# Local attention in another order: the work of each engine in a tile moved, half of the weighing one step later, and a subtraction made by scalar_tensor_tensor

## The reference, cut to what matters

```python
h = shift_token(x)                 # second half of the values from the token before
q, k, v = jnp.split(h @ wqkv, 3, axis=-1)
q = l2norm(q) * qs
k = l2norm(k) * ksc
q, k = rotary_xpos(q, k)           # q * cos * scale + rotate_half(q) * sin * scale, k with 1 / scale
# local_attention: each window of 128 queries sees its own keys and those of the window before
sim = jnp.einsum('bhwid,bhwjd->bhwij', bq, bk)
mask = (i < j) | (i > j + WINDOW) | (j == -1)
sim = jnp.where(mask, -jnp.finfo(sim.dtype).max, sim)
attn = jax.nn.softmax(sim, axis=-1)
out = jnp.einsum('bhwij,bhwjd->bhwid', attn, bv)
x = x + o @ wo
```

## Time and profile before

| | |
|---|---|
| time, median of 3 runs | 4296.58 us (4293.78 to 4302.39) |
| the profiled execution | 4296.06 us, its span 4294.4 us |
| mean granted clock of TensorE | 0.951 of full |
| PE busy | 3835.2 us, 89% |
| DVE busy | 3330.0 us, 78% |
| ACT busy | 2558.9 us, 60% |
| POOL busy | 1191.1 us, 28% |

### The profile page before, as it was taken

One profiled execution on the slowest core, in us unless ns is written; L12 is line 12 of the kernel. 1 busy time (PEld: TensorE's weight loads), 2 busy tenths in 40 slices (PEclk: granted clock), 3 DMA queues, 4 the chain that ended last, 5 costly groups with the idle time before them and its releaser, 6 DMA issues. The chain is left out here.

```text
span 4294.4 us, 94790 instructions
## 1 busy us (share of the span) xinstructions
PE 3835.2 (89%) x38292; PEld 2167.2 (50%) x38292; DVE 3330.0 (78%) x5467; ACT 2558.9 (60%) x3449; POOL 1191.1 (28%) x966
## 2 busy tenths in 40 slices
PE   7999999769998969998986999999999999866996
PEld 4788888535655535555553332332333333334664
DVE  5688988779985569985687889999998978584444
ACT  3566666646553435653443777787888887744553
POOL 1022321267761067771141000000000000033552
PEclk9999999889999989999997999999999999977998
DMA  1010100133330033430072000000000000034664
GB/s 63 5 40 28 43 25 25 41 70 64 63 51 28 0 63 66 65 55 9 0 160 47 9 9 2 9 2 2 9 2 2 9 2 9 4 100 93 117 134 111
DMA packets 325878, 175.39 MB, mean 41 GB/s; under 512 B 239508, under 2 KB 316520, under 8 KB 324968
## 3 DMA queue, kind: packets, MB, share of 16 engines
q1 hardware_dynamic: 302856, 133.88, 14.8%
q0 software_dynamic: 13440, 21.24, 2.9%
q10 hardware_dynamic: 9184, 14.68, 1.4%
HBM read 77.81 MB, written 38.58 MB: 27 GB/s over the span
## 5 line engine op out<-in xcount | busy, mean ns | idle before, releaser
L2257 DVE TENSOR_REDUCE s_tops<-ps 128x2 f32<-128x1024 f32 (+3 forms) x1152 | 1252.2, 1132 | 143.2 <-PE ps L2143 103.6
L2226 ACT ACTIVATE s_weights<-ps 128x1024 f32<-128x1024 f32 (+3 forms) x1152 | 1092.5, 952 | 344.3 <-PE ps L2156 193.8
L2178 PE MATMUL ps<-s_weights,v_flat 128*32 128x256 f32 (+1 forms) x8704 | 692.1, 390 | 7.4 <-ACT s_o_t L2232 6.1
L2137 PE MATMUL ps<-keys,s_q 48*128 48x512 f16 (+3 forms) x2304 | 435.0, 375 | 46.0 <-DVE s_tops L2257 26.0
L2156 PE MATMUL ps<-s_q,keys 50*128 50x512 f16 (+3 forms) x2304 | 434.0, 374 | 46.9 <-DVE s_tops L2257 33.3
L2293 POOL CAST s_shift<-s_minus_top 128x16 f16<-128x16 f32 x32 | 6.3, 196 | 1429.9 <-DVE s_minus_top L2264 1429.9
L583 PE MATMUL ps<-a_qt,a_kt 128*128 128x256 f16 x3072 | 375.3, 273 | 3.8 <-POOL s_ones L538 3.8
L2156 PEld LDWEIGHTS ps<-s_q,keys 50*128 50x128 f16 x2304 | 112.2, 93 | 512.3 <-issue 246.7
L1174 PE MATMUL ps<-attention_w,la_yt 128*128 128x512 f16 x1152 | 289.3, 399 | 37.8 <-DMA la_yt<-la_y_parts 30.3
L583 PEld LDWEIGHTS ps<-a_qt,a_kt 128*128 128x128 f16 x3072 | 300.9, 98 | 40.3 <-POOL s_ones L538 4.2
L1249 ACT ACTIVATE la_weights<-ps 128x1024 f32<-128x1024 f32 x124 | 126.8, 1023 | 291.5 <-PE ps L1164 291.5
(11 more groups left out here) (372 smaller groups left out, 7158.0 us busy)
## 6 DMA issues: line engine op xcount, KB each, us to landing
ex_whole<-in_L_ffn_w_dram ACTq DMA_DIRECT2D x14, 1024.0 KB, 10.2
qk_parts<-a_parts SPq DMA_DIRECT2D x64, 128.0 KB, 4.3
keys<-qk_parts SPq DMA_DIRECT2D x48, 128.0 KB, 5.7
s_q<-qk_parts SPq DMA_DIRECT2D x48, 128.0 KB, 5.0
x<-in_x_dram SPq DMA_DIRECT2D x8, 512.0 KB, 9.3
attention_w<-attention_split SPq DMA_DIRECT2D x2, 2048.0 KB, 9.1
la_table<-in_rotary_dram SPq DMA_DIRECT2D x64, 64.0 KB, 2.1
a_table<-in_rope_dram POOLq DMA_DIRECT2D x8, 512.0 KB, 6.1
```

Source lines behind the costliest of these rows:

```text
L2137: mm = pe.matmul(m.ps[:, bank, 0:width], b.q[rows(half, KEY_PARTS * L1_DH), place % 2, pair, t * P:(t + 1) * P], m.keys[rows(half, KEY_PAR ...
L2178: mm = pe.matmul(m.ps[h * QUAD:(h + 1) * QUAD, OUT, begin:end], m.v_flat[:, first:first + QUAD], weights[:, a % 2, h, begin:end], start=(k ...
L2226: act.activation(weights[:, a % 2, 2 * pair:2 * pair + 2, skip:CHUNK], m.ps[:, bank:end + 1, skip:CHUNK], ACT.Exp).then_inc(s["exp"], 1)
L2257: dve.tensor_reduce(tops[:, u % 2, :, i % 2, t, c], m.ps[:, bank:end + 1, 0:width], AX.X, ALU.max).then_inc(s["max"], 1)
```

## The change

Only the `step` functions of `local_attention` and two operations change:

- PE: `project_q`, `project_k` of a tile come a step earlier and stand last in the step; `weigh(w, 1)` comes a step later, as the second thing of step w + 1, and `project_o` a step later, as the first. `find(i + 2, 1)` moves behind `score(i, 1)`. Between `score(i, 0)` and `score(i, 1)` now stands only `project_v(i + 1)`.
- DVE: `low` and `sums` of a tile come a step later, `divide(w, 0)` too; `rotate` now stands between the two `find`s, and `low` is the first call of a step, behind `find(i + 2, 1)` of the step before.
- `take_shift` goes from DVE to ACT.
- POOL: `add` and `norms` of a tile a step later, right ahead of `normalise`.
- SP: `turn_shift`, `turn_k`, `turn_q` and `place_shift` each work on one tile less ahead. The order in SP's step stays.
- `low` is a scalar_tensor_tensor (times 1.0, minus the high half) instead of a tensor_tensor.
- There is one more step at the end, and the row statistics that hang on a number of finished tiles come a step later.

The diff:

```diff
@@ -931,7 +931,7 @@
     near = m.mask[:, :, :].rearrange("p b k -> p (b k)")
     wqkv = m.attention_w[:, :, 0:KD * 3 * INNER].rearrange("p s (k e) -> p s k e", k=KD)
     wo = m.attention_w[:, :, KD * 3 * INNER:].rearrange("p s (k e) -> p s k e", k=INNER // P)
-    LOAD, HALF_ROWS, DOWN, ROWS, POWER, UP = 2, EARLY_TILES + 1, EARLY_TILES + 2, EARLY_TILES + 4, EARLY_TILES + 5, EARLY_TILES + 6
+    LOAD, HALF_ROWS, DOWN, ROWS, POWER, UP = 2, EARLY_TILES + 2, EARLY_TILES + 3, EARLY_TILES + 5, EARLY_TILES + 6, EARLY_TILES + 7
     early = slice(0, EARLY_TILES)
     with ExitStack() as ctx:
         def sb(name, shape, dt=F32):
@@ -966,7 +966,7 @@
 
         def run(step):
 
-            for i in range(-7, TILES + 2):
+            for i in range(-7, TILES + 3):
                 step(i)
 
         def after(eng, sem, n):
@@ -1036,13 +1036,13 @@
                 def step(i):
                     if exists(i + 5):
                         load_table(i + 5)
+                    if exists(i + 1):
+                        turn_shift(i + 1)
                     if exists(i + 2):
-                        turn_shift(i + 2)
-                    if exists(i + 3):
-                        turn_k(i + 3)
-                        turn_q(i + 3)
-                    if exists(i + 2):
-                        place_shift(i + 2)
+                        turn_k(i + 2)
+                        turn_q(i + 2)
+                    if exists(i + 1):
+                        place_shift(i + 1)
                     if exists(i + 6):
                         turn_y(i + 6)
                     if i == LOAD:
@@ -1108,19 +1108,18 @@
                     pool.tensor_tensor(rnorm[:, :], ss[:, :], m.minus_half[:, 0:2 * HEADS], ALU.pow).then_inc(s["rnorm"], 1)
 
                 def step(i):
-                    if exists(i + 3):
-                        normalise(i + 3)
                     if exists(i + 4):
                         tables(i + 4)
+                    if exists(i + 5) and i + 5 and (i + 5) % RING == 0:
+                        edge(i + 5)
+                    if exists(i + 3):
+                        add(i + 3)
+                        norms(i + 3)
+                        normalise(i + 3)
                     if exists(i - 1):
                         low_o(i - 1)
-                    if exists(i + 5) and i + 5 and (i + 5) % RING == 0:
-                        edge(i + 5)
                     if exists(i + 6):
                         low_y(i + 6)
-                    if exists(i + 4):
-                        add(i + 4)
-                        norms(i + 4)
                     if i == POWER:
                         rows_on_gpsimd(pool, m, s, 0)
 
@@ -1215,25 +1214,25 @@
                     mm.then_inc(s["proj"], 1)
 
                 def step(i):
+                    if exists(i - 2):
+                        project_o(i - 2)
+                    if exists(i - 1):
+                        weigh(i - 1, 1)
                     if exists(i + 2):
                         find(i + 2, 0)
-                    if exists(i + 4):
-                        project_q(i + 4)
                     if exists(i):
                         score(i, 0)
-                    if exists(i + 2):
-                        find(i + 2, 1)
-                    if exists(i + 4):
-                        project_k(i + 4)
                     if exists(i + 1):
                         project_v(i + 1)
                     if exists(i):
                         score(i, 1)
+                    if exists(i + 2):
+                        find(i + 2, 1)
+                    if exists(i):
                         weigh(i, 0)
-                    if exists(i - 1):
-                        project_o(i - 1)
-                    if exists(i):
-                        weigh(i, 1)
+                    if exists(i + 5):
+                        project_q(i + 5)
+                        project_k(i + 5)
 
                 run(step)
 
@@ -1283,29 +1282,36 @@
                     after(act, s["pv"], ROUNDS * (w - SLOTS + 2))
                     act.activation(v[:, w % SLOTS, :], m.ps[:, V_BANK, :], ACT.Copy, scale=1 / SCALE).then_inc(s["v"], 1)
 
+                def take_shift(w):
+                    act.wait_ge(s["top"], ROUNDS * (w + 1))
+                    after(act, s["shift_t"], 16 * (w - 1))
+                    act.activation(shift[:, w % 2, 0:HEADS], top[:, w % 2, :], ACT.Copy, scale=-1.0).then_inc(s["shift"], 1)
+
                 def high_y(w):
                     landed(act, y_in, w - 2)
                     act.copy(y_parts[:, w % 2, 0, :], m.y[:, w, :]).then_inc(s["y_high"], 1)
 
                 def step(i):
-                    if exists(i + 1) and i + 1:
-                        queries_for_before(i + 1)
+                    if exists(i - 1):
+                        soften(i - 1, 1)
+                    if exists(i + 4):
+                        square(i + 4)
+                    if exists(i + 7):
+                        high_y(i + 7)
+                    if exists(i + 3) and i + 3:
+                        keys_before(i + 3)
                     if exists(i):
                         soften(i, 0)
-                    if exists(i + 3):
-                        high(i + 3)
-                    if exists(i + 4):
-                        square(i + 4)
                     if exists(i - 1):
                         high_o(i - 1)
                     if exists(i + 1):
                         take_v(i + 1)
-                    if exists(i + 3) and i + 3:
-                        keys_before(i + 3)
-                    if exists(i):
-                        soften(i, 1)
-                    if exists(i + 7):
-                        high_y(i + 7)
+                    if exists(i + 3):
+                        high(i + 3)
+                    if exists(i + 2):
+                        take_shift(i + 2)
+                    if exists(i + 2) and i + 2:
+                        queries_for_before(i + 2)
 
                 run(step)
 
@@ -1316,6 +1322,7 @@
                 def find(w, r):
                     dve.wait_ge(s["found"], ROUNDS * w + r + 1)
                     after(dve, s["top"], ROUNDS * w + r)
+                    after(dve, s["shift"], w - 1)
                     first = 0 if w else P
                     for g in range(2):
                         for h in range(2):
@@ -1324,15 +1331,10 @@
                                                          1.0, -3e38, ALU.add, ALU.max, top[:, w % 2, n:n + 1])
                     t.then_inc(s["top"], 1)
 
-                def take_shift(w):
-                    dve.wait_ge(s["top"], ROUNDS * (w + 1))
-                    after(dve, s["shift_t"], 16 * (w - 1))
-                    dve.tensor_scalar(shift[:, w % 2, 0:HEADS], top[:, w % 2, :], -1.0, None, ALU.mult).then_inc(s["shift"], 1)
-
                 def low(w):
                     dve.wait_ge(s["high"], w + 1)
-                    dve.tensor_tensor(parts[:, w % 2, :, 1, :], straight[:, w % 2, :].rearrange("p (n e) -> p n e", n=2), parts[:, w % 2, :, 0, :],
-                                      ALU.subtract).then_inc(s["low"], 1)
+                    dve.scalar_tensor_tensor(parts[:, w % 2, :, 1, :], straight[:, w % 2, :].rearrange("p (n e) -> p n e", n=2), 1.0, parts[:, w % 2, :, 0, :],
+                                             ALU.mult, ALU.subtract).then_inc(s["low"], 1)
 
                 def rotate(w):
                     dve.wait_ge(s["squares"], w + 1)
@@ -1378,24 +1380,23 @@
 
                 def step(i):
                     if exists(i + 2):
-                        find(i + 2, 0)
+                        low(i + 2)
+                    if exists(i - 1):
+                        divide(i - 1, 0)
+                    if exists(i + 3):
+                        sums(i + 3)
+                    if exists(i - 3):
+                        halves(i - 3)
+                    if exists(i - 2):
+                        residual(i - 2)
                     if exists(i - 1):
                         divide(i - 1, 1)
                     if exists(i + 2):
-                        find(i + 2, 1)
-                        take_shift(i + 2)
-                    if exists(i + 3):
-                        low(i + 3)
+                        find(i + 2, 0)
                     if exists(i + 4):
                         rotate(i + 4)
-                    if exists(i):
-                        divide(i, 0)
-                    if exists(i + 4):
-                        sums(i + 4)
-                    if exists(i - 2):
-                        halves(i - 2)
-                    if exists(i - 1):
-                        residual(i - 1)
+                    if exists(i + 2):
+                        find(i + 2, 1)
                     if i == HALF_ROWS:
                         dve.wait_ge(s["six"], EARLY_TILES)
                         half_rows_on_vector(dve, m, s, 0)
```

## The result

The changed kernel takes 4450.9 us, the kernel before 4296.7 (medians of four runs each); the ratio over all these runs is 1.0363, 95% interval 1.0347 to 1.0380. It is 154 us slower, where 14 were forecast, and above the range. Nearly all of it is in local attention. From the first to the last score of a layer it takes 460.8 and 452.9 us, before 376.3 and 375.8: 161.6 of the 169.5 us by which the spans of the two profiled executions differ.

The account below looks back on a forecast made before the run. A closed loop over POOL's power, ACT's high and DVE was taken to set the 12.29 us tile. The new SP loop, 12.30 plus 0.4 for late DMAs, gives 12.7; with layer ends +6.8 per layer, +14 in all: 4310 us, range 4275 to 4400.

Parts of the forecast that it names:

- the new loop: Local attention, from score over second find, low, SP's turns and placing to next score: 12.30 us, 12.7 with late DMAs.
- PE's long wait: Sign at PE's score (L1159): waits for band about once a tile, by some tenths to over 1 us.
- Its wait for `la_o`: Sign on PE in the profile after: its wait for la_o is gone.
- race: DVE's low (wants to start at 5.50) against POOL's 2.37 us add (5.59); the sum has low win.
- the sum: Times added from the start of score(i, 0) to the next score, every DMA at its usual speed: 12.30 us.
- It is ahead by 0.09: On DVE and POOL, low at 5.50 us behind the score starts before the add at 5.59.
- Rival 1: Race lost: add first, k's turn on SP at 9.05 not 7.12, 1.93 a tile, 4422 (partly 4340 to 4420); chance 0.22.
- the sum had SP free at 5.89: On SP, the shift's turn starts 5.89 us behind the score, place_shift at 9.86.
- Late DMAs, 0.4 a tile: SP's queue in the loop: one k turn in three late by 0.87, plus late landings, together 0.4 us a tile.
- Ends: Ends of a local attention layer: first score 4.6 us earlier, the last step's low and turns cost about 1.
- scalar_tensor_tensor: no effect: DVE's low in the new form takes 1.23 us, not expected to differ, and is hidden either way.
- `take_shift` on ACT: The shift's write on ACT, without a row: taken as 0.19 us, bounded by 0 and 0.61.

Follow-up runs that it names:

- e5: The changed kernel with POOL's add waiting for low and POOL's low_y ahead of low_o: 4369.7 us, 1.0166 of the kernel before.
- e13: e1 with y's turn and the table's load behind the placing of band on SP, and ACT's high_y a tile earlier: 4357.4 us, 1.0144.
- e2: The changed kernel with eight more matmuls of 512 columns a tile ahead of PE's wait for the turned q: 4433.2 us, 1.0305.
- e1: The changed kernel with POOL's add of a tile waiting for low of the tile before: 4412.5 us, 1.0260 of the kernel before.
- e11: e5 with four more matmuls of 512 columns a tile ahead of PE's wait for the turned q: 4350.1 us, 1.0125.
- e4: The changed kernel with low as a tensor_tensor subtraction again: 4448.5 us, 1.0340 of the kernel before.
- e8: The kernel before with low by scalar_tensor_tensor alone: 4297.2 us, 1.0001 of the kernel before.
- e7: e5 with the second find ahead of the second score on PE, behind the projection of v: 4338.6 us, 1.0088.
- e14: e13 with the second find ahead of the second score and the MLP's loads two a step over four steps: 4327.9 us, 1.0083.
- e16: e14 with DVE's rotate ahead of divide(i - 1, 1) and the first find's maxima: 4311.2 us, 1.0023 of the kernel before.
- e6: The changed kernel with POOL's low_y ahead of low_o alone, the add not waiting for low: 4422.2 us, 1.0290.
- e9: e5 with the second find right behind the first score on PE, ahead of the projection of v: 4344.5 us, 1.0114.
- e10: e9 without POOL's wait for low ahead of the add: 4375.9 us, 1.0181 of the kernel before.

## Why the prediction was wrong, point by point

The direction and the new loop were right: POOL's power waits for DVE, and the loop runs from score over the second find, `low` and SP's queue to the next score. PE's long wait was expected at the score, for `band`; it stands just ahead, at the first find, for q's turn (25.4 us in 200, against 0.9 for `band`). Its wait for `la_o`, expected to go, fell only from 11.0 to 6.5. With race and y's turn out of the way (e5, e13) the loop takes 12.38 us against 12.30 in the sum.

- **The failed step is "It is ahead by 0.09".** The add starts where it was said, 5.59 behind the score. `low` starts at 5.60, not 5.50: from the first score to the next instruction it takes 1.29, where I took the 1.19 of the earlier trace rows. That row has a `find` behind the score; now a projection stands there. The kernel before shows the 1.29 too, where something else follows the score:

```profile
1016.95 0.60 PE L1160 MATMUL ps<-band,spread 128*128 128x256 bf16 x4
...
1018.24 1.08 PE L1205 MATMUL ps<-la_weights,la_v 128*32 128x128 f32 x32
```

It isn't PE's idle time ahead of the score: in e2 the extra matmuls leave none in half of the tiles, and it is 1.29 there as well. The race was lost by 0.00 to 0.02 in the quiet tiles, all but the two behind a copy for the ring's edge. Rival 1 was the case that happened, to the number in a quiet tile: k's turn was put at 9.05 and starts at 9.07. The total is another matter: rival 1 ended at 4422, and 29 more came from the terms below. The error was to give a difference of 0.09, under the spread of its own terms, a chance of only 0.22.
- **A second step failed with it: the sum had SP free at 5.89.** I counted y's turn and the table on SP, but not what releases them: `low_y`, now behind `low_o` on POOL and so behind exp. They move the shift's turn to 6.73, 0.84 a tile. Under the lost race it is hidden; e1 against e5 shows 43 us of it, and e13 against e1 55 by the other way. With the race won but this left as it was, e1 measures 4412.5, still over the range's 4400; e5, without both, has 4369.7 and lies in it. (The 0.03 by which the sum goes from 5.86 to 5.89 has no source either, and is of no weight.)
- **Late DMAs, 0.4 a tile**: in the 28 of the 46 tiles that run at the upper clock, the time from k's turn to the next score is 5.79 in the mean against 5.2 in quiet ones, so 0.59 a tile, where 0.4 was taken. It isn't at k's turn, which takes 1.24 to 1.26 throughout, but in landing: from the start of q's turn until PE has it, it takes 4.3 to 4.8 us in 12 of the 46 tiles and 3.2 to 3.9 in the others. Right in kind, a third too small, and at another DMA than the one that was read.
- **No term for the clock.** By the earlier trace rows it was 1.00 and I left it there, though the new loop makes PE wait before `find`. Taking it away brought 18 to 20 us, what the extra matmuls cost already taken off (e2, e11; e11 is the cleaner one, since it has no race).
- **Ends and the loads.** The first score comes at 911.76 against 911.84, not 4.6 earlier. The race eats that gain too: ahead of the first score `low` takes 3.14 at 890.90 and 2.23 at 904.32. In e1, where it takes 1.22 there, the first score comes at 907.54, 4.3 earlier than before. The first two intervals of a layer cost 11 us over both layers, the tiles with the loads another 11, both unforeseen.
- **scalar_tensor_tensor: no effect**, right (e4, e8). `take_shift` on ACT takes 0.21, where 0.19 was taken.

The account of the 154 as steps from kernel to kernel, each in the order in which it was taken: race 38 (e1), y's turn 43 (e5), second find 31 (e7), then 11 for SP's order and the split loads (e14), and 17 for e16, whose mechanism isn't shown. That is 140, from medians of different rounds (the kernel before has 4296.1 to 4299.7 in them). The rest of 14 (12 against the kernel before in e16's own runs, with a ratio of 1.0023) is open: e16 has a clock of 1.00 in the 200 us and still takes 12.6 a tile against 12.1 before. None of these steps can be read as its value in another order: race and y's turn hide each other (e1, e5, e6), and something on DVE hides the place of the second find (e7, e9); `rotate` stands there, but no run has it out of the way.

## What to carry to other kernels

When an edit breaks the loop that sets the time, list everything that the next instruction in line waits for, on every queue, and what releases each of those, since several may be late at the same place: here `low`, the add and the shift's turn behind y's turn all came due between 5 and 7 us behind the score (5.60, 5.59 and 6.73 in a quiet tile). Where two instructions that contend start within 0.1 us of each other by the sum, price both sides: here the coin fell the same way in 26 of the 28 tiles at the upper clock. Or order them by a wait, which here cost nothing: POOL's power waited 3.8 us for `la_ss` in the changed kernel, and in e1 it still waits 0.2 for it. Price a loop that has a DMA queue in it with its late landings: PE waited 25.4 us in 200 for q here, and 2.2 in the kernel before, whose turns ran a step further ahead. And read a row's distance to the next instruction only for the same next instruction: the 1.19 that was 1.29 lost the race.

## What the runs showed of the hardware that was not expected

- Which of `low` and the add pays changed over 0.10 us in e10: a `low` started 0.04 ahead of the add (1757.29 against 1757.33) takes 1.22 and the add 3.40, one started 0.06 behind it (1701.86 against 1701.80) takes 3.38 and the add 2.37. In the changed kernel a `low` started 0.01 behind the add (983.32 against 983.31) takes 3.44, and one started 0.11 ahead (1926.48 against 1926.59) takes 1.24 and the add 3.35.
- In the changed kernel PE fell to the lower level (a granted clock of 0.51 from 1072.20 to 1075.00) behind an idle stretch of 2.26 us, and the projection that followed took 2.74 for 1.47, while the mean clock of the 200 us still read 0.93. Four matmuls a tile whose results are thrown away gave more than they cost: e11, in which four take 1.04 us at 1036.00, measures 20 us less than e5.
- In the changed kernel the turn of q landed late in 12 of 46 tiles, 4.3 to 4.8 us behind its start instead of about 3.2, while its issue never took over 1.36.
- The write of the shift on ACT takes 0.21 in the changed kernel (L1288); on DVE in the kernel before (L1330, 1000 to 1200 us) it took 0.32 in the mean (0.17 to 0.46).
